# One kernel, four layers: two engines' queues reordered in the dilated attention

## The reference

```python
# SEGMENT = 256, DILATION = 2, k = 128, 16 heads of 16
xs = x[:, global_idx, :]                       # every second row of each segment of 256
qh = xs.reshape(b, n_seg, k, 16, 16)
scores = einsum('bsqhd,bskhd->bshqk', qh, qh) / 4
attn = softmax(scores, axis=-1)
seg_out = einsum('bshqk,bskhd->bsqhd', attn, qh)
# den = sum of a row's output over all 256 columns; alpha = den / den (each row is written once)
x = layernorm(x + seg_out * alpha)             # on the even rows; odd rows keep x
```

## Time and profile before

| | |
|---|---|
| median of 3 runs | 1466.42 us (1463.88 to 1467.57) |
| profiled execution | 1466.65 us, span 1464.9 us |
| TensorE busy | 1346.3 us, 92% of the span |
| VectorE busy | 892.5 us, 61% |
| ScalarE busy | 653.4 us, 45% |
| GpSimd busy | 748.2 us, 51% |
| mean granted TensorE clock | 0.966 |
| last instructions of the attention stage | near 135 us |

### The profile page before, as it was taken

How to read it: one execution, slowest core, us unless ns; L and a number is a source line. 1 busy time by engine, 2 the same in 40 slices (tenths; PEclk the granted TensorE clock), 3 DMA queues, 4 the chain that set the end, 5 groups by cost and what they waited for, 6 DMA issues and landing times. The chain is left out here.

```text
span 1464.9 us, 29291 instructions
## 1 busy us (share of the span) xinstructions
PE 1346.3 (92%) x9425; PEld 1207.5 (82%) x9426; DVE 892.5 (61%) x1856; ACT 653.4 (45%) x1174; POOL 748.2 (51%) x695
## 2 busy tenths in 40 slices
PE   6776798999999994999989999999999988999998
PEld 3444687888888883777778999999999978999997
DVE  4898422233323324677578888888888853566656
ACT  3554333233333331666544543543543435555553
POOL 5773197765550003331049887987987957240400
PEclk8998799999999997999999999999999999999999
DMA  4102325232210003210033274474474487465450
GB/s 169 61 30 84 124 70 171 100 143 109 86 60 14 14 15 114 92 58 1 1 116 94 85 196 129 146 197 128 144 200 129 141 257 255 159 216 187 152 204 32
DMA packets 112543, 171.49 MB, mean 117 GB/s; under 512 B 6400, under 2 KB 97664, under 8 KB 106336
## 3 DMA queue, kind: packets, MB, share of 16 engines
q1 hardware_dynamic: 103456, 156.27, 33.2%
q0 software_dynamic: 3408, 9.31, 2.2%
q10 hardware_dynamic: 5616, 5.11, 1.0%
HBM read 115.22 MB, written 55.44 MB: 117 GB/s over the span
## 5 line engine op out<-in xcount | busy, mean ns | idle before, releaser
L2126 PE MATMUL comb_psO<-hand_parts,comb_eh 128*128 (+1 forms) x1024 | 198.8, 292 | 0.0
L1791 ACT ACTIVATE disp_raw<-disp_psL 128x512 f32<-128x512 f32 x128 | 76.6, 598 | 198.7 <-PE disp_psL L1703 112.1
L1104 DVE TENSOR_TENSOR moe_hs<-moe_psH,moe_act_a 128x512 f32<-128x512 f32 x78 | 50.2, 686 | 177.2 <-PE moe_psH L998 140.2
L2126 PEld LDWEIGHTS comb_psO<-hand_parts,comb_eh 128*128 128x128 f32 x1024 | 157.6, 190 | 0.1
L1703 PE MATMUL disp_psL<-disp_ph,hand_xh 128*128 (+1 forms) x512 | 148.0, 289 | 0.8 <-DVE disp_e L1976 0.8
L2245 DVE TENSOR_TENSOR comb_el<-comb_psT,comb_eh 128x512 fp32r<-128x512 f32 x128 | 88.1, 688 | 94.1 <-ACT comb_eh L2160 92.3
L1703 PE MATMUL disp_psL<-disp_ph,hand_xl 128*128 (+1 forms) x512 | 145.1, 283 | 0.0
L1703 PE MATMUL disp_psL<-disp_pl,hand_xh 128*128 (+1 forms) x512 | 145.0, 283 | 0.0
L2126 PE MATMUL comb_psO<-hand_parts,comb_el 128*128 (+1 forms) x512 | 144.7, 283 | 0.0
L1727 PE MATMUL disp_psS<-disp_e,last_x 128*128 128x256 f32 x512 | 133.6, 384 | 4.3 <-POOL disp_e L1885 4.3
L1202 POOL DMA_INDIRECT lin_yg<-sorted_y,table_place x32 | 32.3, 1011 | 190.0 <-POOLq L913 143.3
(11 more groups left out here) (295 smaller groups left out, 3894.0 us busy)
## 6 DMA issues: line engine op xcount, KB each, us to landing
logits<-disp_raw SPq DMA_DIRECT2D x64, 512.0 KB, 4.1
hand_e<-logits SPq DMA_DIRECT2D x32, 1024.0 KB, 6.5
w_raw<-in_w SPq DMA_DIRECT2D x8, 2048.0 KB
disp_wt<-in_w_slot SPq DMA_DIRECT2D x16, 1024.0 KB, 10.3
w_raw<-in_w SPq DMA_DIRECT2D x8, 1024.0 KB
slot_y<-disp_slots SPq DMA_DIRECT2D x64, 128.0 KB, 3.2
disp_bt<-in_b_slot SPq DMA_DIRECT2D x15, 512.0 KB, 4.9
comb_y_in<-slot_y SPq DMA_DIRECT2D x3, 2048.0 KB, 10.5
```

The source lines that it names most:

```text
L1104: v.tensor_tensor(hs[:, cols], psH[:, 2 + h, :], act_a[:, cols], ALU.mult).then_inc(hs_ready, 1)
L1791: nc.scalar.activation(raw[mc % 4][:, half * 2:half * 2 + 2, :], psL[l_bank[mc]][:, half * 2:half * 2 + 2, :], ACT.Copy).then_inc(copied, 1)
L2126: last = nc.tensor.matmul(psO[j % 2][:, 0:D], ep[s % EB][:, i, :], yp[:, bass.ds(odd, 1), ch * D:(ch + 1) * D].rearrange("p a d -> p (a d) ...
```

## The change

Two `step` functions get another order; nothing is computed otherwise. On ScalarE keep_x goes from behind high to the head of the step, ahead of the exponential. On VectorE low moves ahead of divide; rest_x moves from the head of the next (odd) step to the place behind low in the even step, so that it stands before sum_up; and spread becomes the first piece of every step.

```diff
@@ scalar @@
             def step(i, k):
-                exponent(i, k)
-                high(i, k)
                 at = segment(i, k, -2)
                 if at is not None:
                     keep_x(*at)
+                exponent(i, k)
+                high(i, k)
                 keep_out(i, k)
@@ vector @@
             def step(i, k):
-                at = segment(i, k, -1)
+                spread(i, k)
+                maximum(i, k)
+                finish(i, k)
+                low(i, k)
+                at = segment(i, k, -2)
                 if at is not None:
                     rest_x(*at)
-                spread(i, k)
-                maximum(i, k)
                 divide(i, k)
-                finish(i, k)
-                low(i, k)
                 total(i, k)
                 sum_up(i, k)
```

## The result

The changed kernel takes 1482.17 us (median of 4 runs, 1479.81 to 1483.85), the kernel before 1466.14 on the same chip (1463.88 to 1467.57): a ratio of 1.011, 95% interval 1.009 to 1.0129. It is 16 us slower; 6.5 had been forecast. The profiled execution took 1479.81 us and is the fastest of the four.

What follows compares the result with a forecast made beforehand. A circle of waits bounds the attention stage, in even steps through VectorE's queue ahead of the shift. Loop 4.6, steps 5, 7 and 29 1.2, step 31 0.7: 6.5 us slower, 1473.0 us, range 1468.3 to 1478.0.

Steps and rivals of the forecast that it cites:

- The path: VectorE's queue ahead of the even step's shift: divide behind low delays it 0.84 - 0.38 = 0.46 us per segment.
- the upper bound: Divide behind low, if low ends no earlier: 0.84 us per segment, 11.4 us in all.
- ScalarE's edit: keep_x ahead of the exponential fits into ScalarE's 1.22 us idle time: 0 us; 6.6 us if that cover were gone.
- The collision of low with GpSimd's product: Odd pair's low on VectorE ends when GpSimd's mask product ends; rest_x earlier brings that end from 61.80 to 61.42.
- the clock's: Rival: TensorE's granted clock falls for a third of the loop's twenty steps, adding 8 us: 1481 us; chance 0.04.
- The free order of the rival: Rival: in even steps the transpose binds the shift, VectorE's order is free; 3.2 us gained, 1463.2 us; chance 0.06.

Runs made afterwards that it cites:

- E2: Kernel before with only low moved ahead of divide on VectorE, rest_x and keep_x left in place: 1485.0 us, ratio 1.0132 to before.
- E3: Changed kernel with divide put back ahead of low, rest_x and keep_x where the change puts them: 1463.3 us, ratio 0.998 to before.
- E4: Changed kernel with TensorE's two transposes of x in each even step issued three times over: 1469.3 us, ratio 1.0023 to before.
- E7: Kernel before with the transposes of x in each even step issued three times over, as the control: 1460.3 us, ratio 0.9975 to before.
- E1: Kernel before with only keep_x moved ahead of the exponential on ScalarE, VectorE's old order kept: 1468.4 us, ratio 1.0012 to before.
- E9: Kernel before with only rest_x moved on VectorE, behind low in the even step, ScalarE's old order kept: 1460.6 us, ratio 0.9978 to before.
- E5: Kernel before with one more VectorE reduce of heads, result unused, behind the statistics in each odd step: 1471.7 us, ratio 1.0052 to before.
- E6: E5 with the transposes of x in each even step issued three times over: 1463.6 us, ratio 0.9991 to before.

## Why the prediction was wrong

**The path: right.** Divide lost its hole, the chain behind low grew by 0.84 us, the earlier rest_x took back what it shortened low by. Low's end came 0.47 us earlier instead of 0.38, since rest_x starts 0.09 us behind low and not 0.2, so the cost per segment is 0.40 us, not 0.46. Shown by the steps at 2.4 GHz, by E2 (0.88 without the earlier rest_x; the upper bound said 0.84), and by E3 (nothing lost once divide is back). With the added transposes in both kernels, where the profiled loops show a clock of 0.98 and 1.00, the change costs 1.0023 / 0.9975 = 1.0048, 7 us (E4 against E7; 2 to 12 us if the ends of the two intervals are set against each other), with 6.5 forecast.

**ScalarE's edit: right**, nothing measurable (E1, E9).

**The collision of low with GpSimd's product: right.** Low ended with a product in every version: it took 0.82 us in the kernel before and 0.83 in E2, where rest_x has its old place, 0.35 in the changed kernel, and 0.53 in E9, where rest_x waits for keep_x.

**The step that failed** is the clock's. The prediction listed it as a rival, with the right mechanism and nearly the right price (1481 us; it became 1482), and gave it 0.04 on the sentence "Nothing in the rows shows such a fall at this share". That the price came so near is partly luck: a third of the steps was assumed and not read from a row, at 1.1 us each, while in the changed kernel's loop a fall cost an odd step 0.8 to 1.4 us (4.84 for 3.45 at most) and an even one 0.2 to 0.6. The sum then took every step at 2.4 GHz, and the range ended with the path's upper bound. The runs put in its place: about 9 of the 16 us come from TensorE at 1.2 GHz, because the longer wait for the shift leaves it idle more of the time. Shown by filling part of the idle time and leaving the path (E4: the same 7.46 us for two steps, yet 13 us less, 9 beyond the control, or 1 to 17 if the ends of the intervals are set against each other), and by making the wait longer in another way (E5) or longer still (E2: clock 0.78, the slowest of all). E6 points the same way: 8 us less than E5, some 4 beyond the control, which the times alone don't set apart from noise, but the loop is 4.5 us shorter, where in the control it is unchanged. The loops are those of one execution each, two of the changed kernel. The mean granted clock of the whole program is known for nearly every execution and agrees: 0.952 to 0.966 in eight of the changed kernel, 0.961 to 0.976 in ten of E4, 0.961 to 0.977 in sixty of the kernel before.

What should have raised the chance stood in the prediction itself: TensorE's share of an iteration was put at 74% before and 69% after, and that no row showed a fall at 69% was read as speaking against one, when no row had a share so low at 2.4 GHz for that long. One execution of before with a clock of 1.00 throughout the loop was taken for a stage that is safe. E1 puts that in doubt: with the same path and the same 74% its clock fell twice in the loop, about a microsecond each. That the kernel before can lose its clock there too is likely by that and not shown, since its only profiled execution has no such fall. Its spread doesn't show it either: 25 executions in one session lie between 1460.4 and 1471.1 us, but the ten of E6, whose profiled loop held its clock, spread as widely, from 1458.8 to 1469.6.

**The free order of the rival** was not quite empty. The prediction priced a shift released by its transpose at 3.2 us and asked for divide to lie elsewhere. With divide left where it was, the move of rest_x frees the shift: 2.8 us in the loop together with keep_x (E3), 2.3 by itself (E9).

**Open:** the 4 us that the added transposes give the kernel before outside the loop (E7); at which steps the clock falls in a given execution; and whether TensorE's idle time in all or the length of its single wait makes it fall, since the delays lengthen both and the added transposes shorten both.

## What to carry to other kernels

A wait for another engine is a slot in an in-order queue: work that stands ahead of the waiting instruction is free as far as it fits into the wait, and the same work behind it lands on whatever comes next. Before moving it, ask which of the two sides has the hole.

Where TensorE waits in every step of a stage, price each delay on its path twice, once as its length and once as TensorE at half clock, and look at more than one execution before taking the clock for granted. Here 4.0 us of path in a loop brought 6.8 us of slow clock with them; repeating transposes in idle slots gave back 6.0 us of the loop's time.

## What the runs showed of the hardware

A VectorE instruction of eight columns (0.16 us by itself) took 0.82 us in the kernel before and 1.08 at most (E5) while GpSimd worked on mask products. In the twelve traces it took over 0.2 us 166 times, and each time it ended 0.01 to 0.03 us after a mask product. In the longest case this was not the product that it started in but the next: low started at 95.48, GpSimd's products run from 94.50 to 95.54 and from 95.50 to 96.54, and low ended at 96.56. What set its length was where in GpSimd's 1.00 us rhythm it started, so that moving another VectorE instruction by 0.5 us shortened it by 0.47.

```profile
95.48 1.08 DVE L482 SCALAR_TENSOR_TENSOR att_negmax<-att_mx,att_negmax 128x8 fp32r<-128x8 f32 x1 [0.46 <-ACT att_negmax L390]
```

This is the contention that the Trainium skill ("SBUF — State Buffer", Who interferes with whom) describes, and the trace agrees, with 0.16 against 0.82 us.

In the changed kernel the granted clock fell in single steps of a steady loop, with TensorE busy 5.26 of 7.46 and 5.27 of 7.82 us in the four steps before, and rose again by itself in the same loop: 59.28 to 68.00 at 0.80, the next two steps at 1.00, 109.08 to 118.49 at 0.50. A step at 1.2 GHz throughout took 4.6 to 4.8 us against 3.45 to 4.4 at 2.4.
